# Moving one batch's linear attention into the expert loop, one batch's softplus into the last loop, and the media norm into the context tiles, in a two-layer decoder on one core

## The chip, the cores and the metric

The kernel runs on one core of one Trainium2 chip. The metric is the device time of one execution in microseconds (us). The engines are TensorE (PE, with its weight loads shown apart as PEld), VectorE (DVE), ScalarE (ACT), GpSimd (POOL) and SyncE (SP), which issues the DMAs. Each engine works through its own instructions strictly in their written order; they meet at semaphores.

## The reference, cut to what matters

Two decoder layers on x of 4 batches x 512 tokens x 128 features with a context of 77 rows per batch, all in fp32. Every sublayer is followed by a residual and a layer norm:

```python
x = LN(x + cosine_attention(x))                          # norm "A"
x = LN(x + cross_attention_16_heads(x, ctx))             # norm "B"
x = LN(x + experts(x))                                   # norm "C": 8 routed (top 2) and 1 shared expert, silu(g) * u
q, k, v = split(x @ W_qkv.T)                             # linear attention
q, k = softplus(l2norm(q)), softplus(l2norm(k))          # per head of 8
x = LN(x + (q @ (k.T @ v)) * scale / (q @ sum(k)))       # norm "D"
lat, media = LN(x) * w + b, LN(ctx) * w + b              # norms "lat" and "media"
x = LN(x + softmax(q(lat) @ k([media, lat]).T) @ v(...) @ Wout)   # norm "E", 16 heads of 64, 589 keys
x = LN(x + 3 cycles of a gated twist of x)               # norm "F"
```

Softplus is computed as ln(1 + exp(z)): one pass with Exp and one with Ln on ACT.

## The kernel before, in words

The program is written engine by engine, by hand. No planner orders it: the order is that of the Python loops of each engine, and a few tables of numbers (steps at which something is inserted). Its stages in time:

- **Cosine attention** (0 to about 58 us), batch by batch. Behind it DVE takes the statistics of norm A of batch 3, of the media norm (`norm_stats`), and applies both (`norm_apply`), before the first `max_sub(0)`.
- **Context attention**: 16 "context tiles" `tt` of 128 tokens. Per tile PE makes scores (`scores0`), DVE subtracts the row maxima (`max_sub`, L1074 and L1077), ACT takes Exp, PE transposes and multiplies, DVE divides (`divide0`).
- **Experts**: `e_all` counts 36 steps, 9 for each batch. In a step PE runs `up(e_all + 1)` (12 matmuls for two blocks `n` = 2 * e_all and 2 * e_all + 1 of gate and up projection) and then `down(e_all)`. ACT takes Silu of block n (L839), DVE multiplies (`gate`, L1154) and adds the weighted output (`accumulate`, L1181 or L1178). PE may write the gate projection of block n only when Silu of block n - 2 is done, and its up projection only when the gate multiplication of block n - 2 is done. After the last step of a batch DVE takes norm C and PE transposes the result (`input_d`), one step later PE makes q, k, v (`qkv`), which ACT copies out of PSUM in 12 pieces. The inverse norms of q and k are one POOL power of 20.73 us for each of batches 0, 1, 2 (`invert`, L639).
- **The bridge** (344.8 to 397.1 us), written out piece by piece: softplus of batches 0 and 1, transposes of q (`turn_q`), k.T @ v (`sum_kv`, key `kv`), the outputs of batch 0 (`half_d`, `quotient_d`, key `oD`), its norms D and lat, `qkv` of batch 3, the split of the latents and of the 1024 x 2 columns of Wkv into a rounded leading part and a rest (`split_wide`: ACT writes the lead, POOL the rest), and then the list `PROLOGUE`: projections Q, K, Kt and V of head pair 0, its ten row-maximum units `max`, softplus of batches 2 and 3, `kv` of both, and Q, K, Kt of pair 1. The first score matmul of the last loop comes behind all of this.
- **The last loop**: 32 head pairs p x 10 slots. In a slot PE makes a block of scores (`s_wide`), ACT takes Exp (L941), PE multiplies the Exp of the slot before by V (`pv`). Tasks are hung into slots: projections of pair p + 2 (ACT `hi`, L914, DVE `lo`, L1287, POOL `twins`, L673), maxima of p + 1 (DVE L1343), outputs and norms of the linear attention of batches 1 to 3 (`OD_STEPS`, `NORM_AT`).
- **Epilogue**: the three cycles of the twist.

X and Y alternate as buffers: X_ODD holds the result of norms A, C and E, X_EVEN that of B and D and also q of the linear attention; Y holds k, sums, and later the latents. Every norm needs a power on POOL between statistics and application (`rstd`, L570), and POOL takes them in the order in which `LN_KEYS` and its own list name them.

Two lines say what the placement of the work in the experts rests on:

```python
if n >= 2: pe.wait_ge(silu_ready, n - 1)     # before the gate projection of block n
if n >= 2: pe.wait_ge(h_ready, n - 1)        # before its up projection
```

Of the kernel before, what the change touches and what calls it, by code (L numbers as in the profile page):

```python
# [117 lines left out]
D_INPUT, D_QKV, D_SUMS, D_NORMED = 1, 2, 3, 11  # L118
# [16 lines left out]
def lane_a_tasks():  # L135
# [10 lines left out]
    t += [("qT", 0), ("qT", 1), ("xT", "D", B - 1)] + [("qkv", B - 1, i) for i in range(NT)] + [("latT", 0), ("qT", 2), ("qT", 3)]  # L146
# [13 lines left out]
def lane_v_tasks():  # L160
# [14 lines left out]
    t += [("kv", 0), ("kv", 1)] + [("oD", 0, h) for h in range(2)]  # L175
# [17 lines left out]

OD_STEPS = {(0, 8): (1, 0), (0, 9): (1, 1), (2, 9): (2, 0), (3, 9): (2, 1), (5, 9): (3, 0), (6, 9): (3, 1)}
# [5 lines left out]
def step_tasks(p):  # L200
# [27 lines left out]
def splits(tasks, slot):  # L228
# [26 lines left out]
def decoder(nc, x, ctx, wq0, bq0, wk0, bk0, wv0, bv0, wo0, bo0, w_router, w_g, w_u, w_d, s_g, s_u, s_d, w_qkv,  # L255
# [3 lines left out]
    with es:  # L259
# [264 lines left out]
        def _(pool):  # L524
# [117 lines left out]
            for b in range(B):  # L642
# [3 lines left out]
                if b < B - 1:  # L646
                    invert(b)
# [39 lines left out]
            for key in PROLOGUE:  # L687
                if key[0] in ("Q", "K", "Kt"):
                    twins(key)
                elif key == ("kv", B - 1):  # L690
# [1257 lines left out]
```

## Time and profile before

| what | value |
|---|---|
| median of 3 runs | 1122.23 us (1119.28 to 1124.82) |
| the profiled execution | 1122.65 us, its span 1120.9 us |
| PE busy | 1043.4 us (93%) |
| PEld, DVE, ACT, POOL busy | 888.2, 738.5, 503.5, 248.6 us |
| chain that ended last, by engine | PE 81%, DVE 9%, ACT 4%, POOL 3%, issue 2%, DMA 1% |
| mean granted TensorE clock | 0.977 of 2.4 GHz |

Busy time of PE is modelled from pipelined matmuls. A granted clock of 1.00 is 2.4 GHz, 0.50 is 1.2 GHz. In a timeline row the brackets give the idle time of the engine before the instruction and what ended it.

### The profile page before, as it was taken

To read this page: it belongs to the slowest core of one execution; us is meant where nothing else is said; L and a number is where in the kernel's file an instruction comes from. 1 tells how busy PE (TensorE), PEld (TensorE's weight loads), DVE (VectorE), ACT (ScalarE), POOL (GpSimd) and SP (SyncE) were. 2 spreads that over 40 slices of the span, in tenths; PEclk is the share of its full clock that TensorE was granted. 3 is DMA by queue.
4 is the path that set the end of the run, shared out by engine and by line. 5 is a ranking of instruction groups with operands and counts; after the bars stand their busy time and mean duration, and the time that the engine had idled before them with its cause. 6 is when DMAs were issued, how large, how long until landed. Compare 5 with 4: busy or idle time off the path is not lost.

```text
span 1120.9 us, 18232 instructions
## 1 busy us (share of the span) xinstructions
PE 1043.4 (93%) x6794; PEld 888.2 (79%) x6794; DVE 738.5 (66%) x1736; ACT 503.5 (45%) x933; POOL 248.6 (22%) x308
## 2 busy tenths in 40 slices
PE   6859889999997599999999999999999999999896
PEld 3647678888886478998999999899999899999432
DVE  5867867556566668777767667657676756762257
ACT  4336554333235554544434444435444435443453
POOL 7111400053735222212121111112111111110001
PEclk9969999999999689999999999999999999999998
DMA  7100000000001000000000000000000000000001
GB/s 234 7 1 1 1 1 1 1 1 1 1 1 38 1 1 2 1 2 1 1 2 1 1 1 2 1 2 2 1 2 1 2 1 1 2 1 1 1 1 38
DMA packets 15682, 10.13 MB, mean 9 GB/s; under 512 B 8759, under 2 KB 14827, under 8 KB 15083
## 3 DMA queue, kind: packets, MB, share of 16 engines
q1 hardware_dynamic: 15595, 8.96, 2.8%
q8 instruction: 55, 0.90, 0.3%
q14 instruction: 32, 0.26, 0.1%
HBM read 7.60 MB, written 1.05 MB: 8 GB/s over the span
## 4 chain that ended last, share of the span: by engine, by line
PE 81%; DVE 9%; ACT 4%; POOL 3%; issue 2%; DMA 1%; POOLq 0%; DVEq 0%; ACTq 0%; SPq 0%
PE PS L1458 77%; PE PS L1470 2%; POOL VXA L639 2%; PE PS L1829 1%; DVE BIG L1077 1%; DVE mx L1074 1%; DVE st L983 1%; DVE KB L1287 1%; DVE X_ODD L994 1%; ACT BIG L727 1%; DVE X_EVEN L994 1%; POOL rs L570 0%; ACT XT L727 0%; ACT BIG L757 0%; DMA QB<-crow 0%
## 5 line engine op out<-in xcount | busy, mean ns | idle before, releaser
L1458 PEld LDWEIGHTS PS<-VXA,BIG 128*128 128x128 f32 (+1 forms) x3136 | 400.7, 192 | 26.7
L1458 PE MATMUL PS<-VXA,BIG 128*128 128x65 f32 (+2 forms) x3136 | 395.8, 271 | 0.0
L941 ACT ACTIVATE BIG<-PS 128x512 f32<-128x512 f32 (+1 forms) x320 | 189.8, 593 | 228.9 <-PE PS L1458 228.2
L1343 DVE TENSOR_REDUCE mxm<-PS 128x1 f32<-128x512 f32 x256 | 170.7, 688 | 83.6 <-PE PS L1458 78.7
L1458 PE MATMUL PS<-QA,KA 128*128 128x512 f32 (+1 forms) x320 | 145.4, 454 | 0.3
L1458 PE MATMUL PS<-QB,KB 128*128 128x512 f32 (+1 forms) x320 | 126.1, 394 | 0.0
L1458 PE MATMUL PS<-KA,QA 128*128 128x512 f32 (+1 forms) x512 | 116.2, 330 | 0.7 <-DVE mxm L1343 0.5
L1458 PEld LDWEIGHTS PS<-KA,QA 128*128 128x128 f32 x512 | 87.0, 190 | 21.4 <-DVE mxm L1343 2.3
L673 POOL CAST KA<-KA 64x78 fp32r<-64x78 f32 (+1 forms) x128 | 54.9, 429 | 221.5 <-ACT KA L914 218.0
L914 ACT ACTIVATE KA<-PS,b1s 64x78 fp32r<-64x78 f32 (+1 forms) x128 | 64.3, 502 | 84.5 <-PE PS L1458 82.9
L673 POOL CAST QB<-QA 64x512 fp32r<-64x512 f32 x64 | 39.0, 609 | 257.2 <-ACT QA L914 257.0
L570 POOL TENSOR_TENSOR rs<-ve,half_neg 128x4 f32<-128x4 f32 (+1 forms) x29 | 30.3, 1045 | 258.1 <-DVE ve L988 257.9
L839 ACT ACTIVATE BIG<-PS 128x512 f32<-128x512 f32 x72 | 42.4, 596 | 94.1 <-PE PS L1458 93.8
L639 POOL TENSOR_TENSOR VXA<-VXA,half_neg 128x128 f32<-128x128 f32 x3 | 62.2, 20727 | 49.4 <-DVE VXA L1160 49.4
L1154 DVE TENSOR_TENSOR BIG<-PS,BIG 128x512 f32<-128x512 f32 x72 | 48.6, 689 | 37.0 <-PE PS L1458 22.3
L1287 DVE SCALAR_TENSOR_TENSOR KB<-PS,b1s,KA 64x78 fp32r<-64x78 f32 (+1 forms) x128 | 67.1, 524 | 4.7 <-ACT KA L914 1.2
L1458 PEld LDWEIGHTS PS<-QB,KB 128*128 128x128 f32 (+1 forms) x320 | 58.5, 183 | 5.5
L914 ACT ACTIVATE QA<-PS,b1s 64x512 fp32r<-64x512 f32 x64 | 43.7, 683 | 42.1 <-PE PS L1458 41.3
L1458 PEld LDWEIGHTS PS<-QA,KA 128*128 128x128 f32 (+1 forms) x320 | 58.5, 183 | 5.2 <-DMA QB<-crow 0.7
L1458 PE MATMUL PS<-XHI,UPHI 128*128 128x512 f32 x144 | 60.5, 420 | 0.4 <-DVE BIG L1154 0.4
L1458 PE MATMUL PS<-XLO,UPHI 128*128 128x512 f32 x144 | 57.3, 398 | 0.0
L1458 PE MATMUL PS<-XHI,UPLO 128*128 128x512 f32 x144 | 56.4, 392 | 0.0
(255 smaller groups left out, 1536.3 us busy)
## 6 DMA issues: line engine op xcount, KB each, us to landing
X_EVEN<-in_x SPq DMA_DIRECT2D x4, 256.0 KB, 3.8
VXA<-in_L_ffn_Wg SPq DMA_DIRECT2D x1, 1024.0 KB, 5.8
VXA<-in_L_ffn_Wu SPq DMA_DIRECT2D x1, 1024.0 KB, 7.7
VXA<-in_L_ffn_Wd SPq DMA_DIRECT2D x1, 1024.0 KB, 9.4
REG<-in_L_xattn_Wkv SPq DMA_DIRECT2D x1, 1024.0 KB, 4.8
QB<-crow SPq DMA_DIRECT2D x64, 2.0 KB
out<-X_EVEN SPq DMA_DIRECT2D x4, 256.0 KB, 2.3
wq1s<-in_L_xattn_Wq SPq DMA_DIRECT2D x1, 512.0 KB, 8.3
```

The costliest lines, as they stand in the source:

```text
L570: pool.tensor_tensor(rs[0:rows, n, :], ve[0:rows, n, :], half_neg[0:rows, 0:NT], ALU.pow).then_inc(rstd_ready, 1)
L639: pool.tensor_tensor(SSQ[b], SSQ[b], half_neg[:, 0:1].broadcast_to([P, NSQ]), ALU.pow).then_inc(pow_ready, 1)
L673: pool.tensor_copy(dst, src.bitcast(F32)).then_inc(twin_ready, 1)
L839: act.activation(SG[:, n % 4, :], PS[:, n % 2, :], ACT.Silu).then_inc(silu_ready, 1)
L914: act.activation(dst, PS[own, 6 + n % 2, 0:width], ACT.Identity, bias=bias).then_inc(hi_ready, 1)
L941: act.activation(PX[0:rows, g % 4, :], PS[0:rows, g % 2, :], ACT.Exp, scale=SCALE_W).then_inc(pw_ready, 1)
L994: ins = dve.tensor_scalar(dst[0:rows, t, :], src[0:rows, t, :], mv[0:rows, n, t, 0:1], rs[0:rows, n, t:t + 1], ALU.subtract, ALU.mult)
L1154: dve.tensor_tensor(HX[:, e_all % 3, k, :], PS[:, 2 + n % 2, :], SG[:, n % 4, :], ALU.mult).then_inc(h_ready, 1)
L1287: ins = dve.scalar_tensor_tensor(dst, PS[rows, 6 + n % 2, 0:width], bias, lead.bitcast(F32), ALU.add, ALU.subtract)
L1343: dve.tensor_reduce(mxm[:, p % 2, h, m:m + 1], PS[:, 2 + g % 2, :], AX.X, ALU.max).then_inc(mu_free, 1)
L1458: return pe.matmul(dst, lhsT, rhs, start=start, stop=stop, **kw)
L1470: ins = pe.transpose(bank[0:src.shape[1], rows * n:rows * n + rows], src, ident[0:rows, 0:rows])
```

## The change

The change moves instructions and adds hardly any. (1) Softplus, q transpose, `kv`, `oD` and the norms D and lat of batch 0 leave the bridge and go into expert steps 17 to 30. (2) The bridge then holds softplus of batches 1 and 2, and `PROLOGUE` is mixed anew: `input_d` and `qkv` of batch 3, the turns of q and `kv` of batches 1 and 2, Q, K, Kt of pair 1 between the maxima. (3) Softplus, turn and `kv` of batch 3 go into steps 0, 1 and 2 of the last loop; the turn of its q is now copied by DVE. (4) The media norm moves from before the first context tile into tiles 1 and 2. (5) On PE the first projection waits for three split pieces, no longer five; the wait for five stands before K.

```diff
-           + [("C", b) for b in range(B)] + D_NORMS
+           + [("C", 0), ("C", 1), ("D", 0), ("lat", 0), ("C", 2), ("C", 3)] + D_NORMS
...
-D_INPUT, D_QKV, D_SUMS, D_NORMED = 1, 2, 3, 11
+D_INPUT, D_QKV, D_SUMS = 1, 2, 3
+SCALE_AT = {17: 0, 28: 1, 34: 2}
+SOFT0_EXP, SOFT0_LN = 38, 40
+KV0_AT, OD0_AT, NORM0_AT, LAT0_AT = 21, {22: 0, 23: 1}, {24: [0], 25: [1, 2]}, 30
...
+SCALE_STEP, SOFT_EXP_STEP, SOFT_LN_STEP, KV_STEP = (0, 4), (0, 7), (1, 7), (2, 8)
...
+PROLOGUE = [("Q", 0), ("K", 0), ("Kt", 0), ("input",), ("V", 0, 0), ("max", 0), ("max", 1), ("qkv",), ("V", 0, 2), ("max", 2), ("max", 3),
+            ("turn", 1), ("V", 0, 4), ("max", 4), ("max", 5), ("kv", 1), ("Q", 1), ("V", 0, 6), ("max", 6), ("max", 7), ("K", 1),
+            ("V", 0, 8), ("max", 8), ("squares",), ("max", 9), ("Kt", 1), ("turn", 2), ("c", 0), ("kv", 2), ("roots",)]
...
 @block.gpsimd
+            for b in range(B - 1):
+                if b == 2:
+                    rstd(("D", 0))
+                    rstd(("lat", 0))
                 rstd(("C", b))
...
+            split_lat(0)
             split_wide(3)
             split_wide(4)
-            rstd(("D", 0))
-            rstd(("lat", 0))
-            split_lat(0)
+            rstd(("C", B - 1))
             split_wide(5)
             split_wide(6)
...
 @block.scalar, behind Silu of block n
+                if n == SOFT0_EXP:
+                    soft_exp(0)
+                if n == SOFT0_LN:
+                    soft_ln(0)
+                if n % HB == 1 and e_all == KV0_AT:
+                    evac(("qT", 0), QTD[:, 0, :])
+                if n % HB == 1 and e_all == LAT0_AT:
+                    latents(0)
...
 @block.scalar, in the last loop
+                    if (p, slot) == SOFT_EXP_STEP:
+                        soft_exp(B - 1)
+                    if (p, slot) == SOFT_LN_STEP:
+                        soft_ln(B - 1)
...
 @block.vector
-            dve.wait_ge(ctx_in, 16)
-            norm_stats(("media", 0), ctx_sb, rows=CK)
             norm_apply(("A", B - 1), Y[:, B - 1], xtile("A", B - 1))
-            norm_apply(("media", 0), ctx_sb, ctxn, rows=CK)
...
+                if tt == 1:
+                    dve.wait_ge(ctx_in, 16)
+                    norm_stats(("media", 0), ctx_sb, rows=CK)
+                elif tt == 2:
+                    norm_apply(("media", 0), ctx_sb, ctxn, rows=CK)
...
+                if e_all == max(NORM0_AT) + 1:
+                    latent_norm(3, 0)
+                accumulate(e_all)
+                if e_all == KV0_AT:
+                    gather_lane(0)
...
+                for i in NORM0_AT.get(e_all, []):
+                    latent_norm(i, 0)
...
+                if e_all in SCALE_AT:
+                    scale_qk(SCALE_AT[e_all])
...
 @block.tensor, in the expert loop
+                if e_all == KV0_AT:
+                    turn_q(0)
+                    lane_v(("kv", 0), lambda bank: sum_kv(0, bank))
+                if e_all in OD0_AT:
+                    pe.wait_ge(a_free, LA["qT", 0] + 1)
+                    pe.wait_ge(kvb_ready, 1)
+                    lane_v(("oD", 0, OD0_AT[e_all]), lambda bank: half_d(0, OD0_AT[e_all], bank))
+                if e_all == LAT0_AT:
+                    latents(0)
+
+            pe.wait_ge(v_free, LV["down", B - 1, E] + 1)
             pe.wait_ge(silu_ready, B * EXPERTS * HB)
-            pe.wait_ge(wide_lo, 5)
+            pe.wait_ge(wide_lo, 3)
```

How the order of the instructions moves, at the three places that the prediction speaks of.

**ACT in expert steps 18 to 20.** BIG<-PS is the Silu of a block (the row after XHI begins with block 37), X_EVEN and Y are q and k of batch 0, XT<-PS is the transposed input of batch 1, and the next X_EVEN<-PS begins its `qkv`. Before:

```order
L770 ACTIVATE XHI<-XT 128x512 [waits u_ready,a_free]
L839 ACTIVATE BIG<-PS 128x512 [waits h_ready,g_ready] x3
L727 ACTIVATE XT<-PS 128x512 [waits a_full]
L839 ACTIVATE BIG<-PS 128x512 [waits h_ready,g_ready] x2
L822 ACTIVATE X_EVEN<-PS 128x128 [waits a_full]
```

And now:

```order
L868 ACTIVATE BIG<-PS 128x512 [waits h_ready,g_ready] x2
L850 ACT_TABLE_LOAD
L850 ACTIVATE X_EVEN<-X_EVEN 128x512 [waits qkn_ready]
L851 ACTIVATE Y<-Y 128x512
L868 ACT_TABLE_LOAD [waits h_ready]
L868 ACTIVATE BIG<-PS 128x512 [waits g_ready]
L740 ACTIVATE XT<-PS 128x512 [waits a_full]
L868 ACTIVATE BIG<-PS 128x512 [waits h_ready,g_ready]
L855 ACT_TABLE_LOAD
L855 ACTIVATE X_EVEN<-X_EVEN,ones 128x512 [waits spe_ready]
L856 ACTIVATE Y<-Y,ones 128x512
L868 ACT_TABLE_LOAD [waits h_ready]
```

Exp stands between the Silu of blocks 38 and 39, Ln between those of 40 and 41, each with a table load before and behind.

**POOL at the end of the experts and in the bridge.** VXA<-VXA,half_neg is the power of batch 2's inverse norms, rs are powers of layer norms, LATLO and WKVLO the rests of the latents and of Wkv. Before:

```order
L639 TENSOR_TENSOR VXA<-VXA,half_neg 128x128 [waits ssq_ready]
L570 TENSOR_TENSOR rs<-ve,half_neg 128x4 [waits var_ready]
L618 TENSOR_TENSOR WKVLO<-REG,WKVHI 128x512 [waits wide_hi] x2
L570 TENSOR_TENSOR rs<-ve,half_neg 128x4 [waits var_ready] x2
L623 TENSOR_TENSOR LATLO<-XT,LATHI 128x512 [waits lathi_ready]
```

And now:

```order
L651 TENSOR_TENSOR VXA<-VXA,half_neg 128x128 [waits ssq_ready]
L635 TENSOR_TENSOR LATLO<-XT,LATHI 128x512 [waits lathi_ready]
L630 TENSOR_TENSOR WKVLO<-REG,WKVHI 128x512 [waits wide_hi] x2
L582 TENSOR_TENSOR rs<-ve,half_neg 128x4 [waits var_ready]
L630 TENSOR_TENSOR WKVLO<-REG,WKVHI 128x512 [waits wide_hi] x2
```

The power for norm C of batch 3 stood ahead of the splits of Wkv; it now stands behind two of them and ahead of the other two.

**PE at the first row maxima.** KA,QA are the maxima, WKVHI,LATHI begins a V, wqkvT,XT is `qkv` of batch 3. Now:

```order
L1487 MATMUL PS<-KA,QA 128x512 [waits pj_free,twin_ready]
L1487 MATMUL PS<-KA,QA 128x512
L1487 MATMUL PS<-wqkvT,XT 128x384 [waits a_free,vx_ones]
L1487 MATMUL PS<-wqkvT,XT 128x384 [waits a_free] x3
L1487 MATMUL PS<-WKVHI,LATHI 128x512 [waits wide_lo,latlo_ready,pj_free]
```

`qkv` of batch 3 stood ahead of the whole prologue; it now stands between the first two maxima and the second V.

## Rows read from the trace of the kernel before

**Rows 1.** Windows by stage: us, busy of PE, PEld, DVE, ACT, POOL, PEclk, DMA, GB/s

```profile
344.80:397.10 52.30, 32.35 (x155) 24.16 (x154) 34.55 (x98) 31.37 (x57) 17.76 (x21) 0.80 0.06 21
```

**Rows 2.** Timeline before the first context tile: start, us, instruction, idle before

```profile
57.87 1.01 POOL L570 TENSOR_TENSOR rs<-ve,half_neg 128x4 f32<-128x4 f32 x1 [4.73 <-DVE ve L988]
...
59.08 3.02 DVE L994 TENSOR_SCALAR X_ODD<-Y,mv,rs 128x128 f32<-128x128 f32 x4
...
62.02 1.10 DVE L994 TENSOR_SCALAR VXA<-ctx_sb,mv,rs 77x128 f32<-77x128 f32 x4
```

**Rows 3.** Timeline of expert steps 17 to 19

```profile
262.87 0.60 ACT L839 ACTIVATE BIG<-PS 128x512 f32<-128x512 f32 x1 [0.80 <-PE PS L1458]
...
264.10 2.05 DVE L994 TENSOR_SCALAR X_ODD<-Y,mv,rs 128x128 f32<-128x128 f32 x4 [1.12 <-POOL rs L570]
266.07 1.28 DVE L1154 TENSOR_TENSOR BIG<-PS,BIG 128x512 f32<-128x512 f32 x2
266.21 0.66 PE L1470 MATMUL PS<-ident,X_ODD 128*128 128x128 f32 x4 [0.89 <-DVE X_ODD L994]
...
269.48 1.95 PE L1458 MATMUL PS<-VXA,BIG 128*128 128x128 f32 x16
```

**Rows 4.** DVE and ACT instructions grouped, 344.7 us to the last loop: busy us, mean ns

```profile
L1170 DVE TENSOR_TENSOR X_EVEN<-X_EVEN,VXA 128x512 f32<-128x512 f32 x1 | 0.7, 691 | 0.0
...
L868 ACT ACTIVATE X_EVEN<-X_EVEN,ones 128x512 f32<-128x512 f32 x4 | 2.9, 715 | 0.0
...
L868 ACT ACT_TABLE_LOAD x2 | 2.6, 1283 | 0.0
L863 ACT ACTIVATE X_EVEN<-X_EVEN 128x512 f32<-128x512 f32 x4 | 2.5, 622 | 0.0
```

**Rows 5.** Timeline, weight loads of the pieces that PE is given elsewhere

```profile
388.84 0.42 PEld L1470 LDWEIGHTS PS<-ident,X_EVEN 128*128 128x128 f32 x4
...
390.25 0.97 PEld L1458 LDWEIGHTS PS<-VXA,Y 128*128 128x128 f32 x8
...
417.32 0.55 PEld L1458 LDWEIGHTS PS<-KVB,XT 128*128 128x128 f32 x4
```

**Rows 6.** Timeline of norm C of batch 2, expert steps 26 and 27

```profile
309.80 1.11 DVE L994 TENSOR_SCALAR X_ODD<-Y,mv,rs 128x128 f32<-128x128 f32 x4 [1.12 <-POOL rs L570]
...
310.96 0.66 PE L1470 MATMUL PS<-ident,X_ODD 128*128 128x128 f32 x4
```

**Rows 7.** Timeline of the bridge, 344.8 to 397.1 us

```profile
355.04 2.51 POOL L618 TENSOR_TENSOR WKVLO<-REG,WKVHI 128x512 fp32r<-128x512 f32 x2 [2.04 <-ACT WKVHI L833]
...
369.54 1.12 PE L1470 MATMUL PS<-ident,Y 128*128 128x128 f32 x4 [8.56 <-DVE Y L994]
...
375.99 1.51 DVE L1287 SCALAR_TENSOR_TENSOR QA<-PS,b1s,QA 64x512 fp32r<-64x512 f32 x2 [6.50 <-ACT QA L914]
...
380.55 1.05 PE L1458 MATMUL PS<-KA,QA 128*128 128x512 f32 x2
...
390.55 0.28 DVE L1308 TENSOR_SCALAR crow<-PS 8x128 f32<-8x128 f32 x1 [0.45 <-PE PS L1824]
...
397.13 0.77 PE L1458 MATMUL PS<-QA,KA 128*128 128x512 f32 x1
```

**Rows 8.** DMA issues: KB each, us to landing

```profile
out<-X_EVEN SPq DMA_DIRECT2D x4, 256.0 KB, 2.3
```

**Rows 9.** Timeline of pair 1, slots 8 and 9 of the last loop

```profile
437.22 0.60 ACT L941 ACTIVATE BIG<-PS 128x512 f32<-128x512 f32 x1 [1.46 <-PE PS L1458]
...
438.77 1.00 PE L1458 MATMUL PS<-VXA,BIG 128*128 128x65 f32 x8
```

**Rows 10.** Windows of 2 us, columns as in rows 1

```profile
348.00:350.00 2.00, 0.39 (x4) 0.20 (x2) 1.47 (x3) 1.97 (x3) 0.00 (x0) 1.00 0.47 197
...
352.00:354.00 2.00, 2.00 (x11) 2.00 (x11) 0.96 (x4) 0.76 (x3) 1.00 (x1) 0.50 0.00 0
...
402.00:404.00 2.00, 2.00 (x12) 1.86 (x11) 1.90 (x3) 0.72 (x2) 0.61 (x2) 0.73 0.00 0
```

More of the change, by code:

```diff
@@ L145, in lane_a_tasks @@
         t += [("xT", "D", b)] + [("qkv", b, i) for i in range(NT)]
-    t += [("qT", 0), ("qT", 1), ("xT", "D", B - 1)] + [("qkv", B - 1, i) for i in range(NT)] + [("latT", 0), ("qT", 2), ("qT", 3)]
+        if b == 1:
+            t += [("qT", 0)]
+    t += [("latT", 0), ("xT", "D", B - 1)] + [("qkv", B - 1, i) for i in range(NT)] + [("qT", 1), ("qT", 2)]
     t += [("xT", "F", b) for b in range(B - 1)]
@@ L174, in lane_v_tasks @@
             t += [("cb1",)]
-    t += [("kv", 0), ("kv", 1)] + [("oD", 0, h) for h in range(2)]
+        if e_all == KV0_AT:
+            t += [("kv", 0)]
+        if e_all in OD0_AT:
+            t += [("oD", 0, OD0_AT[e_all])]
     for c in range(CYCLES):
@@ L924, in _ @@
                         hi(key, h)
-                elif key[0] == "soft":
-                    for b in range(2, B):
-                        soft_exp(b)
-                    for b in range(2, B):
-                        soft_ln(b)
-                elif key[0] == "qT":
-                    evac(key, QTD[:, key[1], :])
+                elif key[0] == "input":
+                    evac(("xT", "D", last), XT[:, last, :])
+                elif key[0] == "qkv":
+                    qkv(last)
+                elif key[0] == "turn":
+                    evac(("qT", key[1]), QTD[:, key[1], :])
+                elif key[0] == "roots":
+                    roots()
             for p in range(STEPS):
@@ L1255, in latent_norm, with gather_lane @@
                     apply_d(("lat", b))
-            for b in range(2):
+            def gather_lane(b):
                 n = LV["kv", b]
@@ L1367, in _ @@
                         lo(key, h)
-                elif key[0] in ("soft", "qT"):
-                    continue
-                else:
+                elif key[0] == "squares":
+                    sum_squares(B - 1)
+                elif key[0] not in NO_PROJ:
                     task(key)
@@ L1677, in qkv, with turn_q, sum_kv, latents @@
                     lane_a(("qkv", b, t), lambda bank: mm(bank[:, 0:3 * D], XT[:, b, P * t:P * t + P], wqkvT[:].rearrange("p k n -> p (k n)")))
+            def turn_q(b):
+                pe.wait_ge(sp_ready, b + 1)
+                lane_a(("qT", b), transposes([QD[:, b, t, :] for t in range(NT)]))
+            def sum_kv(b, bank):
+                for t in range(NT):
+                    ins = mm(bank[:, 0:D + 1], KD[:, b, t, :], VXv[:, b, t, :], start=t == 0, stop=t == NT - 1)
+                return ins
+            def latents(b):
+                pe.wait_ge(x_ready, LN["lat", b] + 1)
+                lane_a(("latT", b), transposes(tiles_of(LAT[:, b])))
+            def half_d(b, h, bank):
+                for t in range(2):
+                    tt = 2 * h + t
+                    ins = mm(bank[:, (D + NH) * t:(D + NH) * (t + 1)], QTD[:, b, P * tt:P * tt + P], KVB[:, b, :])
+                return ins
             pe.wait_ge(s0_sub, TILES)
@@ L1808, in task @@
                     ins = product(bank[0:rows, :], hi, lo, WKVHI[:, cols], WKVLO[:, cols])
+                elif kind == "qT":
+                    pe.wait_ge(sp_ready, key[1] + 1)
+                    for t in range(NT):
+                        ins = pe.transpose(bank[:, P * t:P * t + P], QD[:, key[1], t, :], ident[:])
                 elif kind == "kv":
+                    pe.wait_ge(sp_ready, key[1] + 1)
                     ins = sum_kv(key[1], bank)
@@ L1840, in _ @@
                     max_unit(0, key[1])
-                elif key[0] == "soft":
+                elif key[0] == "input":
+                    input_d(B - 1)
+                elif key[0] == "qkv":
+                    qkv(B - 1)
+                elif key[0] == "turn":
+                    turn_q(key[1])
+                elif key[0] in ("squares", "roots"):
                     continue
-                elif key[0] == "qT":
-                    turn_q(key[1])
                 else:
```

175 lines of the change are left out of this document (71 added, 104 removed).

## The prediction

> **What bounds the kernel now.** I read the granted clock and the busy slices of the page first, then the windows by stage, then the timelines of the stages that the change touches. PE carries the chain through the experts and the last loop, at nearly full share. The exception between them is the bridge: in its 52.3 us PE is busy for 32.35 at a mean clock of 0.80 [rows 1], and the longest hole is 8.56 us in front of the latents of batch 0 [rows 7], which have to pass DVE, POOL and ACT one after another. So a piece of work taken out of the bridge can be worth its latency, and one put into the experts or the last loop costs at least what PE spends on it. "Same" below means within 0.5% (5.6 us) of 1122.23, about what a measurement of this kernel can tell from no change. The sum is made against the profiled execution, 1122.65 us, which is 0.4 above the median.
>
> **1. Media norm, -3.0 us.** The power of norm A of batch 3 begins on POOL at 57.87 and takes 1.01, so its application could begin at 58.9 [rows 2]. It begins at 59.08, behind the media statistics, and takes 3.02 instead of the 1.11 of the same four instructions in a quiet place [rows 2, 6]; the application of the media norm ends about 63.0, and only then comes the first `max_sub`, for which PE has been waiting. Now POOL's next power is that of the media norm, whose statistics come two tiles later, so its residual additions are held back behind it and nothing of POOL runs beside DVE: 58.9 + 1.1 = 60.0 instead of 63.0. In the tiles DVE gets 1.4 and 1.1 us more. I cost these at nothing: there the other engines' turns (transposes, Exp, products) end later than DVE's. Without that cover they would take 2.5 back.
>
> The Trainium skill ("GPSIMD Engine Reference", "2. Architecture") says that POOL's physical SBUF ports are shared with DVE; the 3.02 against 1.11 agrees. By that rule a DVE application beside POOL's splits is slow again, which comes back in term 4.
>
> **2. Softplus of batch 0 in the experts, +4.0 us.** Exp stands on ACT between the Silu of blocks 38 and 39. Before, Silu 39 ran at 262.87 [rows 3]. Exp now waits for `scale_qk(0)`, which DVE takes behind norm C of batch 1. That application ends at 264.10 + 2.05 = 266.15 [rows 3]; two products of 0.69 [rows 4], overlapping a little, end at 267.4. Exp of q and k, about 1.15, ends at 268.6; a table load of 1.28 and the Silu of 0.60 [rows 3, 4] end at 270.5. PE has finished its transposes at 266.6 and needs the gates behind the same products: its second block's gate projection waits for Silu 39, so `down(19)` begins at 270.5 + 0.1 + two projections of 0.7 = 272.0 where it began at 269.48 [rows 3]: +2.5. Then Silu 40 ends at 271.6, a load, Ln of q and k (0.72 + 0.62), a load and Silu 41 at 276.15. Only behind it ACT empties the banks of `qkv`, whose third tile PE could send off at about 275.2 and now at 276.7: +1.5.
>
> This is priced from loads of 1.28 [rows 4]. The Trainium skill ("ScalarE: Activation LUTs", "Table sets: the hidden batching unit") asks that calls be batched by table set and prices a switch at about 2.7 us in its example there (the same page gives 1283 ns as measured elsewhere); the change does the opposite, it adds two pairs of loads. By 2.7 the term would be near +8; the rows say 1.28, and I take them.
>
> **3. PE's own work in the experts, +2.9 us, and norm C of batch 2, +1.7 us.** PE is full there, so each piece counts: two turns at 0.42, `kv` 0.97, two halves of `oD` at 0.55 [rows 5], together 2.9. On DVE the norms D and lat of batch 0 sit in steps 24 to 26. Step 26 carries two gates (1.4), the lat application (1.1), the addition and statistics of norm C (2.2), POOL's power with its hand-over (1.1) and the application (1.1). Replayed from step 24 on, with everything 6.5 later by the terms before, the application of norm C ends at 319.1, where 310.9 + 6.5 = 317.4 [rows 6] would do, and PE's transposes wait: +1.7. Lower bound 0, if gates slip less than I count.
>
> **4. The bridge, -6.9 us.** In the time of before: ACT loads the Exp table to 346.05, takes batch 1, waits for `scale_qk(2)` (349.1), ends Exp at 350.3, loads, ends four Ln at 354.15, then writes four leads of Wkv, one each 0.52. POOL takes about 1.25 for each rest [rows 7]: two are done at 357.4, and only then comes the power for norm C of batch 3, to 358.4. DVE waits for it in front of everything else in the prologue: this is the new stall that takes the hole's place. Its application runs beside the last two rests and is stretched as in term 1: to 361.6. Then `lo` of Q 1.51 [rows 7] to 363.1, of K to 364.6, V, and the first maximum at 366.2 instead of 380.55: -14.3.
>
> From the first maximum to the first score it took 397.13 - 380.55 = 16.6 [rows 7]. Now added on the way: `qkv` of batch 3 between the maxima, 2.7 that DVE has nothing to do in; the squares of batch 3 (1.5) and Kt of pair 1 (0.7) on DVE, in front of the row maxima's transpose; and the landing of `crow`. `crow` was written at 390.55 and hidden behind 6.3 us of prologue; now only `kv` of batch 2 is behind it. The trace has no landing for it; the nearest DMA takes 2.3 [rows 8], with the issue 2.6. Sum 7.5, so 16.6 + 7.5 = 24.1, and the first score at 390.3 instead of 397.1: -6.9 (ends -12 and -3, as the additions hide in each other or don't).
>
> **5. The last loop, +3.0 us.** Turn and `kv` of batch 3 are PE work of 0.42 + 0.97 [rows 5] in a full loop: +1.4. Ln at (1, 7) blocks ACT for a load, 1.34 and a load back, from 435.8 to 439.7. The Exp that ran at 437.22 ends at 440.4, and the `pv` that began at 438.77 [rows 9] waits for it: +1.6. Exp at (0, 7) needs no load and delays by less than PE's distance to it, so nothing; `scale_qk(3)` and the q copy on DVE likewise, which has a third of its time free there.
>
> Sum: -3.0 + 4.0 + 2.9 + 1.7 - 6.9 + 3.0 = +1.7 against 1122.65, so 1124.35; 0.4 off for the median: **1124.0 us**. Its own range is 1119 to 1128.
>
> **Rival A: the clock falls with the new waits (slower), 1130.5 us.** Before, PE was busy 0.39 of the 2 us from 348, and from 352 ran at half clock though fully busy [rows 10]; the low stretch took 3.4 us. In steps 18 to 20 PE now rests some 5 us in 12. Two such stretches there cost half each, 3.4. At the first scores the clock was low till about 403.3 (0.73 in the window from 402) [rows 10], 6.2 us after the start; the prologue is now thinner for PE in its last 9 us (3 us of work), and the low stretch may last 9, as after the 8.56 hole: +1.4, and `qkv` of batch 3 at half clock +1.7. Together 6.5. It decides if PEclk falls below 1.00 at the steps 18 to 20. The experts hold 1.00 throughout before, so no row there shows it. Chance 0.28.
>
> The Trainium skill ("TensorE: Matmul & The Clock Gate", Part 1) says that the throttled state is the default and activity releases it. The row at 352 agrees; by that rule this rival is no accident but the usual price of holes.
>
> **Rival B: the prologue overlaps fully (faster), 1115.0 us.** If the application of norm C isn't stretched (-2.0) and the added pieces hide under the maxima as V does, so that 24.1 stays near 17.5 (-7), the sum is 1115. For it: PE, ACT and DVE each are idle for a part of the prologue before. Against it: DVE's own additions alone are 2.2, and the landing of `crow` has nothing to hide behind. Chance 0.17.
>
> **Rival C: the media move brings nothing, 1127.0 us.** The first tile could turn out to wait for another thing by 60 us, or DVE's 2.5 us come back in tiles 1 and 2. For it: DVE is nearly the bound of the tiles. Chance 0.05.
>
> **How the numbers follow.** Forecast 0.50, A 0.28, B 0.17, C 0.05. The range 1115 to 1131.5 reaches to A and B, with the bounds of terms 3 and 4 inside. "Slower" (above 1127.8) takes A, half of C and a small end of the forecast, 0.32; "faster" (below 1116.6) takes B, 0.16; "same" is the rest, 0.52.
>
> **What would show it.** Term 1: the first `max_sub` 3 us earlier. Term 2: Silu 39 about 7.6 us later than before, PE holes of 1.8 and 1.5 us around it. Term 3: a longer PE wait for X_ODD behind step 27. Term 4: DVE idle for about 7 us until POOL's power at 358 (plus some 8.6 us of expert shift), the first maximum 14 us after that of before minus the shift, 24 us from first maximum to first score. Term 5: one PE wait for the Exp of ACT at (1, 8). The prediction is wrong if the bridge gains over 10 us, or if the expert stage grows by under 5 or over 12.

## The result and the profile after

| | before | after |
|---|---|---|
| median of 16 runs | 1122.93 us (1119.28 to 1124.98) | 1125.03 us (1123.60 to 1126.79) |
| span of the profiled execution | 1120.9 us | 1123.4 us |
| experts, power of norm C of batch 1 to the last `down` | 81.59 us | 89.45 us |
| bridge, last `down` to the first score | 52.48 us | 42.82 us |
| last loop and epilogue | 723.8 us | 732.2 us |

The ratio is 1.0021 with a 95% interval of 1.0012 to 1.0031: 2.1 us slower by the medians, within 0.5%. Here and below, ratios and intervals are taken over fast runs alone, without one run of `media_alone` at 3248.84 us and one of the kernel before at 3612.31 us. Behind the small number stand four large ones. Against the kernel before, the profiled execution gains 4.2 us until norm C of batch 1, loses 7.9 in the experts, gains 9.7 in the bridge and loses 8.5 in the last loop and the epilogue: -4.2 + 7.9 - 9.7 + 8.5 = +2.5.

Before the first context tile, the timeline of after (start, us, instruction, idle before) has the application of norm A at 1.11 us where it took 3.02 [rows 2]:

```profile
58.18 1.01 POOL L582 TENSOR_TENSOR rs<-ve,half_neg 128x4 f32<-128x4 f32 x1 [4.73 <-DVE ve L1009]
59.22 1.11 DVE L1015 TENSOR_SCALAR X_ODD<-Y,mv,rs 128x128 f32<-128x128 f32 x4 [1.12 <-POOL rs L582]
60.25 1.43 DVE L1092 TENSOR_REDUCE mx<-PS 128x16 f32<-128x1232 f32 x1
```

In steps 17 to 19, Exp waits on ACT for `scale_qk(0)`, and Silu 39 and 41 wait for their table loads. `down(19)`, at 269.48 before [rows 3], begins at 267.86; with the 4.2 us that were won until there, that is 2.5 us late:

```profile
263.23 0.63 ACT L850 ACTIVATE X_EVEN<-X_EVEN 128x512 f32<-128x512 f32 x1 [4.02 <-DVE Y L1193]
...
264.40 1.28 ACT L868 ACT_TABLE_LOAD   x1
...
265.69 0.60 ACT L868 ACTIVATE BIG<-PS 128x512 f32<-128x512 f32 x1
...
266.34 0.50 PE L1487 MATMUL PS<-XHI,UPHI 128*128 128x512 f32 x1 [1.53 <-ACT BIG L868]
...
267.86 1.95 PE L1487 MATMUL PS<-VXA,BIG 128*128 128x128 f32 x16
...
272.39 1.56 PE L1487 MATMUL PS<-wqkvT,XT 128*128 128x384 f32 x4 [1.29 <-ACT VXA L837]
```

Behind step 26, PE waits for the application of norm C of batch 2, for which it did not wait before [rows 6]:

```profile
313.06 1.12 DVE L1015 TENSOR_SCALAR X_ODD<-Y,mv,rs 128x128 f32<-128x128 f32 x4 [1.12 <-POOL rs L582]
...
314.24 0.66 PE L1499 MATMUL PS<-ident,X_ODD 128*128 128x128 f32 x4 [1.34 <-DVE X_ODD L1015]
```

The bridge as one window (us, busy of PE, PEld, DVE, ACT, POOL, PEclk, DMA, GB/s), to be held against [rows 1]. PE does 7.35 us less in it, and it is 9.6 us shorter:

```profile
348.50:391.20 42.70, 25.00 (x120) 18.06 (x118) 27.96 (x59) 23.41 (x46) 16.41 (x21) 0.79 0.07 25
```

Its timeline. DVE waits 7.02 us for POOL's power, which stands behind two rests of Wkv, and then applies the norm in 3.36 us beside the other two. The first maximum runs at 369.91 instead of 380.55 and the first score at 391.16 instead of 397.13 [rows 7]:

```profile
358.46 2.49 POOL L630 TENSOR_TENSOR WKVLO<-REG,WKVHI 128x512 fp32r<-128x512 f32 x2 [6.80 <-ACT WKVHI L846]
...
361.96 3.36 DVE L1015 TENSOR_SCALAR X_ODD<-Y,mv,rs 128x128 f32<-128x128 f32 x4 [7.02 <-POOL rs L582]
...
369.91 0.79 PE L1487 MATMUL PS<-KA,QA 128*128 128x512 f32 x2
...
388.34 0.28 DVE L1332 TENSOR_SCALAR crow<-PS 8x128 f32<-8x128 f32 x1
...
391.16 0.77 PE L1487 MATMUL PS<-QA,KA 128*128 128x512 f32 x1 [0.71 <-DMA QB<-crow]
```

Where the last loop loses is seen when the 320 Exp of both kernels are set side by side by number. Counted from 0, Exp 6 of after starts 7.6 us before the Exp of the same number in the kernel before (its twin), Exp 8 only 4.7, Exp 24 3.4, Exp 32 1.4, and there it stays up to the last, Exp 319. So three places lose 2.9, 1.4 and 1.95 us, after 1.65 were won at the start of the loop (6.0 ahead at the first score, 7.6 from Exp 2 on), where the clock is back at full 3 us behind the first score instead of 6. The first is pair 0, slots 4 to 7: `scale_qk(3)` makes DVE late, PE waits, and behind the wait its clock is at 0.50. Timeline, then windows of 2 us:

```profile
403.32 1.06 DVE L1193 TENSOR_TENSOR X_EVEN<-X_EVEN,BIG 128x512 f32<-128x512 f32 x1
404.31 0.68 DVE L1193 TENSOR_TENSOR Y<-Y,BIG 128x512 f32<-128x512 f32 x1
...
406.77 1.40 DVE L1311 SCALAR_TENSOR_TENSOR KB<-PS,b1s,KA 64x512 fp32r<-64x512 f32 x3
407.58 0.27 PE L1860 MATMUL PS<-ident,cmx 128*8 128x128 f32 x1 [1.12 <-DVE KB L1311]
...
411.54 0.69 DVE L1323 COPY VXA<-PS 128x512 f32<-128x512 f32 x1 [3.06 <-PE PS L1487]
```

```profile
404.00:406.00 2.00, 2.00 (x18) 1.91 (x17) 1.98 (x4) 0.83 (x3) 0.33 (x2) 1.00 0.00 0
406.00:408.00 2.00, 0.88 (x7) 0.66 (x6) 1.88 (x6) 0.41 (x1) 0.17 (x1) 0.95 0.00 0
408.00:410.00 2.00, 2.00 (x10) 1.88 (x9) 0.45 (x2) 1.29 (x3) 0.00 (x0) 0.50 0.00 1
410.00:412.00 2.00, 2.00 (x10) 1.68 (x9) 0.46 (x1) 0.46 (x1) 0.00 (x0) 0.70 0.02 5
```

The second is the Ln at (1, 7), which answers to [rows 9]; the third is PE's own work on turn and `kv` at (2, 8):

```profile
433.70 1.28 ACT L958 ACT_TABLE_LOAD   x1
...
435.00 1.08 ACT L958 ACTIVATE BIG<-PS 128x512 f32<-128x512 f32 x2
435.65 1.11 PE L1487 MATMUL PS<-VXA,BIG 128*128 128x65 f32 x8 [1.46 <-ACT BIG L958]
```

The other 3.9 us of this execution are lost in the epilogue, at instructions that the change does not touch. PE has the same waits there in both, but here its clock falls (after, then before):

```profile
1050.00:1058.00 8.00, 6.75 (x11) 2.58 (x10) 1.73 (x3) 2.32 (x5) 0.00 (x0) 0.50 0.00 0
```

```profile
1050.00:1058.00 8.00, 6.19 (x17) 2.18 (x16) 3.10 (x7) 4.18 (x7) 0.00 (x0) 1.00 0.00 0
```

Of the 14 profiles of this study, this one and that of `bridge_order` have such a stretch of about 10 us at 0.50, two more (`scale_later` at 1032, `scale0_early` at 1036) a short one of about 4 us soon behind the last Exp, and ten none, so it comes and goes. How much of the median rests on such stretches isn't shown: the profiled execution, at 1125.16 us, is no outlier, and without its 3.9 us it would be under the fastest of the 16 (1123.60).

Times of one kernel differ by 5 us and more between runs, and the clock moves with them: an execution of `media_alone` took a span of 1114.3 us at a mean granted clock of 0.980, another 1120.5 at 0.975. Below I use for each kernel the mean over its runs of span x (1 - clock), the microseconds that the clock fell short of full: 26.7 before (26.2 and 26.8 in the other two sets of its runs), 25.3 after. The rest of the span is then 1094.5 before and 1098.1 after. By this split the change costs 3.6 us of work and waits and wins 1.4 of clock.

The split is bookkeeping and overstates the clock. Among the runs of one and the same kernel, one microsecond more of span x (1 - clock) goes with only about half a microsecond more span (0.3 in after, 0.5 to 0.6 before, 0.5 over all 227 runs whose clock is on record). A likely reason, not tested, is that part of the time at half clock is spent where PE waits anyway.

### The profile page after: what moved, and what is told of

Its sections match the earlier page's. It is cut to its first block, busy times and chain, and to the rows that moved or that the text cites. A ratio compares the mean times of both kernels' runs of the same rounds, so it can differ in the third digit from the quotient of the medians.

```text
span 1123.4 us, 18240 instructions
## 1 busy us (share of the span) xinstructions
PE 1046.4 (93%) x6794; PEld 889.6 (79%) x6794; DVE 740.5 (66%) x1737; ACT 508.2 (45%) x936; POOL 248.9 (22%) x308
## 4 chain that ended last, share of the span: by engine, by line
PE 79%; DVE 10%; ACT 4%; POOL 3%; issue 2%; DMA 1%; POOLq 0%; SPq 0%; DVEq 0%; ACTq 0%
PE PS L1487 75%; PE PS L1499 2%; POOL VXA L651 2%; PE PS L1865 1%; DVE BIG L1095 1%; DVE mx L1092 1%; DVE st L1004 1%; DVE X_ODD L1015 1%; ACT BIG L770 1%; ACT BIG L740 1%; POOL rs L582 1%; DVE X_EVEN L1015 1%; DVE KB L1311 1%; DVE Y L1204 0%; DMA QB<-crow 0%
## 5 line engine op out<-in xcount | busy, mean ns | idle before, releaser
L582 POOL TENSOR_TENSOR rs<-ve,half_neg 128x4 f32<-128x4 f32 (+1 forms) x29 | 29.9, 1032 | 265.9 <-DVE ve L1009 265.7
```

The source lines that it names most:

```text
L582: pool.tensor_tensor(rs[0:rows, n, :], ve[0:rows, n, :], half_neg[0:rows, 0:NT], ALU.pow).then_inc(rstd_ready, 1)
```

## The experiments

Ratios are to the kernel before. The changed kernel stands at 1.0021.

**The media norm alone**, in the kernel before.

```diff
-            dve.wait_ge(ctx_in, 16)
-            norm_stats(("media", 0), ctx_sb, rows=CK)
             norm_apply(("A", B - 1), Y[:, B - 1], xtile("A", B - 1))
-            norm_apply(("media", 0), ctx_sb, ctxn, rows=CK)
...
+                if tt == 1:
+                    dve.wait_ge(ctx_in, 16)
+                    norm_stats(("media", 0), ctx_sb, rows=CK)
+                elif tt == 2:
+                    norm_apply(("media", 0), ctx_sb, ctxn, rows=CK)
```

> The kernel before with the media norm's move alone. If the prediction's term holds (the first max_sub 3.0 us earlier and nothing more), the time is 3.0 us under the kernel before (ratio 0.9973), and the scores of tile 4 and norm C of batch 1 come 3.0 us earlier. If what the changed kernel's trace shows is the media move's own doing (first max_sub -2.8, but the scores of tile 4 and the power of norm C of batch 1 -4.2, because PE's clock comes back to full earlier), all of the rest is shifted by 4.2 us and the ratio is 0.9963. If the media norm costs DVE time in tiles 1 and 2 that is seen later, the shift shrinks to about 1 by the experts (0.999).

Measured: 1120.41 us, 0.9978 (0.9965 to 0.9990), so 2.5 us. In the profile the first `max_sub` is at 60.20 (before 63.04) and the power of norm C of batch 1 at 258.84 (before 263.06): 4.2 us, as in the changed kernel. But in `power_first`, whose program is that of the changed kernel up to there, the low stretch at the first scores lasts until 72.4 instead of 66.5, nearer to the kernel before (75.4), and the same power comes at 260.12: 2.9 us. Over the ten profiles with this order of work up to there it comes 1.4 to 4.2 us earlier than before, the first `max_sub` 2.1 to 2.9. So the move is worth about the 3.0 us of the prediction, and the 1.2 us on top differ from one execution to the next, with the clock.

**scale_qk(0) one step earlier**, with the same table loads in the same places.

```diff
-SCALE_AT = {17: 0, 28: 1, 34: 2}
+SCALE_AT = {16: 0, 28: 1, 34: 2}
```

> The changed kernel with scale_qk(0) behind step 16 instead of 17, everything else as it is. It divides the 3.8 us of the softplus in the experts: Exp then stands on ACT in the same place, with the same table loads, but has nothing to wait for. Theory: the wait of 4.02 us goes, Silu 39 comes about 2.8 us earlier and the 2.5 us before down(19) come back; the 1.3 us of the Ln in front of the qkv banks stay. Power of norm C of batch 1 to the next long power (22.38 us in the changed kernel, 18.59 before): about 19.9; ratio to the changed kernel 0.998. Rival: the loads and passes alone hold Silu 39 and 41 up; then the distance stays at 21.5 to 22.4. Second rival: the 1.4 us of products in front of the gates of step 17 make norm C of batch 1 later, nothing is won.

Measured: 1123.78 us, 1.0008 (0.9997 to 1.0019), 1.5 us under the changed kernel, not clear of the noise. From the power of norm C of batch 1 to the next long power (20.73 us, for batch 1) it takes 19.16 us, where it was 22.38 in after and 18.59 before. So 3.2 of the 3.8 us were the wait for `scale_qk(0)`, and the four loads and four passes cost 0.6. Exp has nothing to wait for any more (timeline of this kernel):

```profile
258.63 1.28 ACT L850 ACT_TABLE_LOAD   x1
259.92 0.63 ACT L850 ACTIVATE X_EVEN<-X_EVEN 128x512 f32<-128x512 f32 x1
...
262.39 0.60 ACT L868 ACTIVATE BIG<-PS 128x512 f32<-128x512 f32 x1
```

That the whole time wins only 1.5 us goes with a larger share of the clock, 27.8.

**The softplus of batch 0 later.**

```diff
-SOFT0_EXP, SOFT0_LN = 38, 40
-KV0_AT, OD0_AT, NORM0_AT, LAT0_AT = 21, {22: 0, 23: 1}, {24: [0], 25: [1, 2]}, 30
+SOFT0_EXP, SOFT0_LN = 43, 45
+KV0_AT, OD0_AT, NORM0_AT, LAT0_AT = 22, {23: 0, 24: 1}, {24: [0], 25: [1, 2]}, 30
```

> The changed kernel with Exp of batch 0 behind Silu 43 instead of 38, Ln behind Silu 45 instead of 40, and turn, kv, oD and the norm D one step later. Theory: the 3.8 us lost in steps 18 to 20 come from Exp waiting 4.02 us on ACT for scale_qk(0) behind norm C of batch 1 (Silu 39 2.8 us late) and from Ln standing in front of the emptying of the qkv banks; later, Exp waits for nothing and no bank waits for it, so 2.5 to 3.8 us come back, ratio to the changed kernel 0.997 to 0.998. Rival: the cost is that of the table loads and passes themselves (2.4 and 3.9 us of ACT in the way of the Silu), which stay wherever they stand: 0 us, and PE shows waits for Silu 44 and 46 instead. A second rival: norm C of batch 2 then collides with the norms of batch 0 in step 26 and takes 1 to 2 us back.

Measured: 1123.31 us, 1.0006 (0.9993 to 1.0019), 1.7 us under the changed kernel, again not clear of the noise. The same distance is 19.35 us, but here it ends at 278.91, and the load for Ln begins only at 279.26. Up to the power of norm C of batch 2, with all four loads inside, it takes 50.46 us, where it was 53.13 in after and 49.91 in `scale0_early`: 2.7 come back, by another way than above. Between 258 and 298 us PE waits for no Silu. So the rival that the loads themselves cost this time has fallen twice.

**scale_qk(3) where DVE is idle.**

```diff
-SCALE_STEP, SOFT_EXP_STEP, SOFT_LN_STEP, KV_STEP = (0, 4), (0, 7), (1, 7), (2, 8)
+SCALE_STEP, SOFT_EXP_STEP, SOFT_LN_STEP, KV_STEP = (0, 7), (1, 2), (1, 7), (2, 8)
```

> The changed kernel with scale_qk(3) moved from (0, 4) to (0, 7), where DVE is idle for 3.06 us, and Exp of batch 3 from (0, 7) to (1, 2). Theory: the two products of scale_qk(3) make DVE late at (0, 6), PE waits 1.1 us at 406.5 for K's rest and the row maxima, and behind this hole it runs at half clock from 407.9 to 411.9; without them both go, the Exp of (1, 0) comes 2.9 us earlier against that of (0, 4), ratio to the changed kernel 0.9974, to the kernel before about 0.9995. Rival 1: only the hole of 1.1 us goes, the clock falls there anyway: 1.1 us. Rival 2: the products collide with the V copy at (0, 7) or Exp of batch 3 with the Exp of (1, 3), and the wait only moves: 0 to -1 us.

Measured: 1120.72 us, 0.9993 (0.9980 to 1.0007), 3.1 us under the changed kernel by the ratios. The wait of 1.12 us and the low stretch at 408 are both gone; Exp 2 to Exp 17 all run 6.7 us before their twins in the kernel before.

**The Ln where PE has most work in hand, and where it has least.** Both start from `scale_later`.

```diff
-... = (0, 7), (1, 2), (1, 7), (2, 8)
+... = (0, 7), (1, 2), (2, 2), (2, 8)
```

> scale_later with the Ln of batch 3 moved from (1, 7) to (2, 2). The seven profiles with both PE holes in the loop (1.1 us at (0, 7), 1.5 us at (1, 7)) each show one stretch of half clock behind one of them, worth 1.2 to 3.2 us. Theory: at slot 2 PE has the most work between an Exp and the product that needs it, and the block of two loads and two passes (3.9 us) fits in front of it (0.1 us left over); the wait of 1.5 us goes and there is no low stretch in the loop. 1.4 us from the hole alone, and up to 3 more in the runs of scale_later in which the clock fell there: ratio to scale_later 0.997 to 0.9987. Rival: the block makes Exp of slots 3 and 4 and ACT's part of K late, and PE waits for those: 0 or slower.

Measured: 1118.96 us, 0.9964 (0.9950 to 0.9978), 2.0 us better than `scale_later` by the medians against the kernel before, 3.3 by the ratios. In the profile the hole's 1.4 us come back whole (Exp 16 to 22 stay 5.4 us ahead of their twins). The block of loads and passes is the same 3.9 us; the product behind it no longer waits (timeline):

```profile
442.65 1.28 ACT L958 ACT_TABLE_LOAD   x1
443.95 0.60 ACT L958 ACTIVATE BIG<-PS 128x512 f32<-128x512 f32 x1
```

```profile
444.64 1.07 PE L1487 MATMUL PS<-VXA,BIG 128*128 128x65 f32 x8
```

With `SOFT_LN_STEP` = (2, 5) instead, and Exp and `scale_qk(3)` as in the kernel above:

> The opposite of ln_slot2: the same kernel with the Ln at (2, 5), where PE's next product stands 1.06 us behind its Exp. Theory: the hole grows from 1.5 to about 3.5 us, so 3.5 us more than ln_slot2, and the clock falls to half behind it in the profile, another 1.5 to 3.5 us. Rival: the low stretches in the loop have nothing to do with the holes; then only the 3.5 us and no low stretch between 400 and 460.

Measured: 1123.88 us, 1.0007 (0.9996 to 1.0018), 4.8 us worse than at slot 2. In the profile 6.8 us are lost between Exp 16 and 32 where `ln_slot2` loses 2.0. The hole is there, and the low stretch behind it:

```profile
453.07 1.11 PE L1487 MATMUL PS<-VXA,BIG 128*128 128x65 f32 x8 [3.37 <-ACT BIG L958]
```

```profile
454.00:456.00 2.00, 2.00 (x12) 1.91 (x12) 0.00 (x0) 0.60 (x1) 0.00 (x0) 0.63 0.00 0
456.00:458.00 2.00, 2.00 (x11) 1.67 (x10) 0.69 (x1) 0.00 (x0) 0.00 (x0) 0.52 0.00 0
```

**POOL's power in front of the rests.**

```diff
+            rstd(("C", B - 1))
             split_wide(3)
             split_wide(4)
-            rstd(("C", B - 1))
```

> The changed kernel with POOL's power of norm C of batch 3 in front of the rests 3 and 4 of Wkv. Theory: DVE's wait of 7.02 us behind its statistics (ready at 354.9) goes, the application runs at about 356 beside an idle POOL (1.1 instead of 3.36 us), lo of Q begins at 361.2 behind ACT's lead instead of 365.35, and the first maximum comes as early as K's own way allows: K's product begins at 361.10 as before, its lead on ACT at 362.8, lo of K at 364 instead of 366.9, the first maximum at about 366.7 instead of 369.9: -3.2 us there, and at the first score between -3.2 and 0, since qkv, the maxima and DVE's squares stand between. Rival: the prologue is bound by its own work from there on and the gain is gone by the first score: 0 us. Second rival: the clock falls earlier in the prologue.

Measured: 1122.30 us, 0.9994 (0.9983 to 1.0005), 3.0 us under the changed kernel. The application takes 1.12 us. From the first lead of Wkv to the first maximum it is 9.2 us (after 12.1), to the first score 32.3 (after 33.4): of 2.9 us at the first maximum 1.1 are left at the first score. The 1.8 are lost between the first pair of maxima and the second (6.0 us instead of 4.2), where PE makes `qkv` of batch 3 and where the low clock, which ends at 370.2 in after, ends at 372.7 here.

**ACT's leads in front of the Ln, in addition.**

```diff
             for b in range(1, 3):
                 soft_exp(b)
-            for b in range(1, 3):
-                soft_ln(b)
...
             for n in range(3, 7):
                 split_wide(n)
+            for b in range(1, 3):
+                soft_ln(b)
```

> power_first, and ACT writes the four leads of Wkv before the Ln of batches 1 and 2, not behind them. Theory: K's product, which waits 6.67 us for POOL's rests, begins 3.7 us earlier, the Ln pass (3.9 us) then stands between the leads and ACT's part of Q and K, so the first maximum comes 2 to 3 us earlier than in power_first (its frame: 9.2 us behind the first lead there). The DVE-bound maxima behind it take no less, so the gain arrives at the first score nearly whole: 2 us. Rival: the longer stretch at half clock takes it back, as in power_first, where the first maximum won 2.9 us and the first score 1.1. Then under 1 us, and the share of low clock in 368 to 374 is what differs.

Measured: 1120.26 us, 0.9979 (0.9968 to 0.9989), about 2 better than `power_first`, as expected. Counted from POOL's power, the first score comes 33.1 us later instead of 35.0. But the first maximum wins only 1.2 us (10.8 instead of 12.0), less than the 2 to 3 expected: the application of the norm now runs beside four rests and takes 5.15 us:

```profile
357.75 4.95 POOL L630 TENSOR_TENSOR WKVLO<-REG,WKVHI 128x512 fp32r<-128x512 f32 x4
```

```profile
357.82 5.15 DVE L1015 TENSOR_SCALAR X_ODD<-Y,mv,rs 128x128 f32<-128x128 f32 x4 [1.12 <-POOL rs L582]
```

**The Ln behind ACT's parts of Q, K and Kt, in addition.**

```diff
             for n in range(3, 7):
                 split_wide(n)
-            for b in range(1, 3):
-                soft_ln(b)
...
                 elif key[0] == "input":
+                    for b in range(1, 3):
+                        soft_ln(b)
                     evac(("xT", "D", last), XT[:, last, :])
```

> leads_first with the Ln of batches 1 and 2 behind ACT's parts of Q, K and Kt of pair 0. Theory: ACT no longer stands in front of Q and K; the first maximum comes another 3 us earlier than in leads_first. But the Ln (3.9 us) then holds up the emptying of the transposes of norm C of batch 3 and qkv behind it, so the second pair of maxima waits about 3 us and most is given back: 0 to 2 us against leads_first at the first score. Rival: PE has a hole of 3 us there, runs at half clock behind it and the first score is later than in leads_first.

Measured: 1127.52 us, 1.0033 (1.0017 to 1.0048), 7.3 us worse than `leads_first` by the medians. The first maximum comes 10.8 us behind POOL's power, as in `leads_first`, so nothing was won there: DVE's long application, not ACT, stood in front of `lo`. The second pair of maxima comes 9.4 us behind the first instead of 5.3, and the clock stays low until 377.6. From POOL's power to the first score it takes 37.2 us instead of 33.1, so the profile loses 4.1 us in the bridge. The rival decided, and the main expectation was wrong in both halves.

**The squares of batch 3 behind crow.**

```diff
-            ("V", 0, 8), ("max", 8), ("squares",), ("max", 9), ("Kt", 1), ("turn", 2), ("c", 0), ("kv", 2), ("roots",)]
+            ("V", 0, 8), ("max", 8), ("max", 9), ("Kt", 1), ("turn", 2), ("c", 0), ("squares",), ("kv", 2), ("roots",)]
```

> The changed kernel with the squares of batch 3 (1.22 + 0.49 us on DVE) behind crow instead of in front of the last maxima. Theory: DVE carries the way from the first maximum to crow, so crow and the first score come 1.5 us earlier (21.25 us from first maximum to first score becomes 19.7), and the roots on ACT, 1.5 us later, still end before the first product with V needs the first Exp. Ratio to the changed kernel 0.9987. Rival: the roots hold up the first Exp, and the 1.5 us come back behind the first score. Second rival: PE, not DVE, carries that stretch, then crow moves by under 0.5 us.

Measured: 1121.66 us, 0.9992 (0.9981 to 1.0002), 3.3 us under the changed kernel. From the first maximum to the first score it takes 20.05 us instead of 21.25; the clock is the likely rest: `kv` of batch 2 runs at full clock and so do the first scores, where after has 0.50 until 394. The clock's share falls to 21.7.

**All that helped, together** (`scale0_early`, `leads_first`, `squares_last`, `ln_slot2`).

> All that helped in one kernel: scale_qk(0) behind step 16, POOL's power of norm C of batch 3 and ACT's leads of Wkv in front, squares of batch 3 behind crow, scale_qk(3) at (0, 7), Exp at (1, 2), Ln at (2, 2). If the gains add up: from the changed kernel's 1125.0 about -1.3 (scale0_early), -4.8 (leads_first), -3.4 (squares_last), -4.3 (scale_later) and -2 (ln_slot2) give 1109. Where they share the same low stretches they do not add: then 1112 to 1116. Either is under the kernel before (1123.0) by more than its interval.

Measured: 1108.86 us, 0.9870 (0.9853 to 0.9886), 14.4 us faster than the kernel before and 16.5 than the changed one. The gains added up (1109 was expected from the sum). The clock's share is 16.6, the rest 1090.8: of 13.8 us against before the split gives 10.1 to the clock. At half a microsecond of span for each, as among the runs of one kernel, that would be about 5 (an estimate). Beside [rows 1] the bridge is:

```profile
348.00:385.70 37.70, 24.87 (x121) 17.86 (x119) 29.36 (x59) 22.75 (x46) 16.80 (x21) 0.86 0.08 29
```

and from 380 to 400, over the start of the loop, PEclk is 1.00; before, the 8 us from 396 have 0.57 (together, then before):

```profile
380.00:400.00 20.00, 16.76 (x109) 14.69 (x110) 16.21 (x34) 10.46 (x19) 4.87 (x10) 1.00 0.00 1
```

```profile
396.00:404.00 8.00, 7.38 (x24) 5.81 (x25) 4.33 (x10) 4.49 (x7) 3.54 (x7) 0.57 0.00 0
```

**crow in front of Kt as well.**

```diff
-("max", 9), ("Kt", 1), ("turn", 2), ("c", 0), ("squares",), ("kv", 2), ("roots",)]
+("max", 9), ("turn", 2), ("c", 0), ("squares",), ("Kt", 1), ("kv", 2), ("roots",)]
```

> together, with the row maxima's transpose and crow in front of Kt of pair 1 and of the squares. Theory: the landing of crow (2.8 us from crow to the first score) is then hidden by Kt, kv of batch 2 and its own wait goes (1.63 us in squares_last); the first score comes 1 to 1.6 us earlier than in together. Rival: DVE's squares are what the roots and the first Exp wait for, and the gain is lost behind the first score: 0.

Measured: 1111.36 us, 0.9889 (0.9871 to 0.9907), 2.5 us worse than `together`, where a gain of 1 to 1.6 or, by the rival, nothing was expected. PE now waits 2.4 us for the row maxima and 1.3 for crow, close to each other, the first score comes no earlier behind the first maximum (19.97 us, in `together` 20.00), and the clock falls where `together` has 1.00:

```profile
382.00:390.00 8.00, 6.69 (x25) 5.57 (x26) 4.37 (x11) 5.08 (x9) 2.84 (x5) 0.57 0.00 1
```

## Why the prediction was right in the sum, and where its steps failed

- **Term 1, media norm**: -3.0 predicted, -4.2 in the profile, -2.5 (-3.9 to -1.1) by the runs of the move alone. The mechanism (POOL beside DVE) is shown by the 1.11 us; the 1.2 us on top come and go between executions, with the clock.
- **Term 2, softplus in the experts**: +4.0 predicted, +3.8 measured, and in the two parts that were named: 2.5 in front of `down(19)`, the rest in front of `qkv`. `scale0_early` shows that both hang on one wait. I had put the second part down to the Ln; it goes with the first. Against the rule of the Trainium skill ("ScalarE: Activation LUTs", "Table sets: the hidden batching unit"), four more loads cost PE 0.6 us here once they did not wait for DVE. Each took 1.28 us in the trace, not the 2.7 of that page's example, and the Silu began right behind it (264.40 and 265.69).
- **Term 3**: +4.6 predicted, +4.1 measured (3.65 to norm C of batch 2, and the turn of the latents). PE's wait behind norm C was 1.34 us where I said 1.7.
- **Term 4, the bridge**: -6.9 predicted, -9.7 measured. The first maximum came 14.3 us earlier against the end of the experts, as the sum had it, with the new wait (7.02 us predicted as 7) and the stretched application (3.36 us predicted as about 3.2). The step that was mis-sized is the way from there to the first score, 24.1 predicted and 21.25 measured. The landing itself was as predicted (2.82 us from crow to the score), but the pieces in front of crow took 18.4 us, not the 21.5 that my sum leaves for them. About 1.1 of that is a double count: the 16.6 us that the sum starts from hold two `kv`, and one of them now runs while crow lands, so that PE waits only 0.71 us for the landing. What hides the other 2 us no run separates. The rows of `kv` before, then the one after:

```profile
390.36 1.05 PE L1458 MATMUL PS<-VXA,Y 128*128 128x129 f32 x8
...
394.44 1.16 PE L1458 MATMUL PS<-VXA,Y 128*128 128x129 f32 x8 [1.19 <-DVE QA L1287]
```

```profile
388.36 2.09 PE L1487 MATMUL PS<-VXA,Y 128*128 128x129 f32 x8
```

- **Term 5, the last loop**: +3.0 predicted, +6.3 measured in the three places. Its Ln was right (1.4 against 1.6) and turn and `kv` nearly (1.95 against 1.4). The step that failed reads "`scale_qk(3)` and the q copy on DVE likewise [nothing], which has a third of its time free there". The third is an average (DVE is busy for 428.3 of the 627 us from 403 to 1030 before); in slots 4 to 6 of pair 0 DVE has hardly a gap, and its idle time, 1.46 us before and 3.06 us after, lies in front of the V copy at slot 7. `scale_later` shows it: 3.1 us.
- **Rival A**, the clock: it was said to decide if PEclk fell at steps 18 to 20. There it held 1.00, and of the eight profiled kernels that keep the wait for `scale_qk(0)` one (`leads_first`) shows 0.62 for 4 us. The clock fell instead behind the small holes in the full loop. All seven profiled kernels that have both holes, 1.1 us at (0, 7) and 1.5 us at (1, 7), show one low stretch in the loop behind one of the two; `ln_slot5` shows one behind its 3.4 us; `scale_later`, with the 1.5 us alone, shows none, and the five kernels with no hole there none either. So the price of such a hole was its length and up to 3.2 us more. With one profile for each kernel this is a pattern of 14 executions, not a rule. The mechanism of the rival was real, its place was wrong.
- **Rivals B and C** did not come: the bridge gained 9.7 us, not the 15.9 that B adds up to (2.9 of its 7 us did hide; its other 2, an application that isn't stretched, did not), and the media move stood. The bridge came close to the 10 us at which the prediction called itself wrong.

Against the profiled execution, terms 1 to 5 were off by -1.2, -0.2, -0.5, -2.8 and +3.3 us, together -1.4. Two pieces of clock that no term had, -1.65 at the start of the loop and +3.9 in the epilogue, add 2.2: 1.7 - 1.4 + 2.2 = 2.5. So the sum was met partly by luck: the bridge and the last loop were each off by about 3 us, in opposite directions. Left open: why in one execution the clock falls in the epilogue and in another not, and which of the two holes in the loop it falls behind.

## What to carry to other kernels

A wait moved into a full loop can cost more than its length. Ask for each block what work the bounding engine has in hand at that very slot, not what share of time the helper is idle: the same 3.9 us on ACT caused no wait at slot 2, and the kernel with them at slot 5 was 4.8 us slower. And where a kernel alternates between a thin stretch and full loops, count the time at low clock for each version over all runs: it fell by 10.1 us in the best version, which was 13.8 us faster. It isn't a sum of time lost, though; compare it with the spread among runs of one kernel first.

## What was not expected of the hardware

- The four `tensor_scalar` of a norm (128x128, fp32) took 1.12 us with POOL idle, 3.36 beside two `tensor_tensor` of 128x512 on POOL and 5.15 beside four; 2.05 beside a single one of 1.27 us [rows 3]. DVE's time grew with POOL's busy time, up to 4.6 times, while POOL's own instructions kept their 1.25 us each.
- One kernel's runs differ by 6 to 8 us without a change in the program: spans of 1114.3 and 1120.5 us at a mean granted clock of 0.980 and 0.975 in `media_alone`, 1119.7 and 1127.3 us at 0.981 and 0.970 in `bridge_order`. The clock goes with the time, but not one to one: 5.7 of the 6.2 us of the first pair stand in span x (1 - clock), and over all runs it takes 2 us of that for 1 us of span.
